# An attention and expert kernel: the second part of its queries, keys and values from a transposed input, and its products of weights and values in twelve sets

## What is computed

```
n = layernorm(x)
q, k, v = Wq n, Wk n, Wv n                    # 16 heads of 16
p = softmax(causal(q k^T / 4))                # per batch and head: 1024 x 1024
x = x + layernorm(Wo (p v))
h = layernorm(x)
w, e = top_2(softmax(h router + bias))
f_e(h) = down_e(act(gate_up_e h + bias_e)) + bias_e
x = x + layernorm(sum over the two experts of w f_e(h))
```

## Time and profile before

| | |
|---|---|
| median of three runs | 1973.35 us |
| profiled execution | 1972.61 us, span 1970.9 us |
| PE busy | 1843.2 us, 94% |
| DVE busy | 1541.8 us, 78% |
| ACT busy | 1310.9 us, 67% |
| POOL busy | 865.1 us, 44% |
| chain that ended last: PE | 84% |

### The profile page before, as it was taken

One profiled execution on the slowest core, in us unless ns is written; L12 is line 12 of the kernel. 1 busy time (PEld: TensorE's weight loads), 2 busy tenths in 40 slices (PEclk: granted clock), 3 DMA queues, 4 the chain that ended last, 5 costly groups with the idle time before them and its releaser, 6 DMA issues.

```text
span 1970.9 us, 75491 instructions
## 1 busy us (share of the span) xinstructions
PE 1843.2 (94%) x26766; PEld 1280.2 (65%) x26767; DVE 1541.8 (78%) x5221; ACT 1310.9 (67%) x3291; POOL 865.1 (44%) x1247
## 2 busy tenths in 40 slices
PE   6899999999999999999999899999999999999980
PEld 3245555555545555455444369999999999999970
DVE  3888888888888888888888658778777777777767
ACT  5177788888888888888787766554445445554437
POOL 4333343445545555555454744544333333333336
PEclk9799999999999999999999999999999999999995
DMA  7744657475655656465557569889899999998848
GB/s 203 219 120 131 196 171 213 150 208 183 184 172 170 189 154 203 137 192 158 167 163 234 169 206 279 240 250 265 252 260 264 257 264 261 264 262 245 239 119 342
DMA packets 255062, 411.72 MB, mean 209 GB/s; under 512 B 34480, under 2 KB 191920, under 8 KB 247600
## 3 DMA queue, kind: packets, MB, share of 16 engines
q1 hardware_dynamic: 217856, 363.46, 57.7%
q0 software_dynamic: 27120, 35.40, 10.2%
q10 hardware_dynamic: 9792, 8.93, 1.5%
HBM read 284.83 MB, written 122.28 MB: 207 GB/s over the span
## 4 chain that ended last, share of the span: by engine, by line
PE 84%; DVE 6%; ACT 4%; issue 3%; DMA 2%; SPq 1%; POOL 0%; DVEq 0%; ACTq 0%; POOLq 0%
PE ps_s L1544 18%; PE ps_s L1375 12%; PE ps_o L1428 12%; PE ps_e L1375 11%; PE ps_w L1375 11%; PE ps_e L1544 6%; PE ps_e L1561 6%; PE ps_o L1561 6%; DVE cmax L792 2%; ACT space L1275 2%; PE ps_e L1554 1%; ACT arena L1167 1%; DVE space L128 1%; PE ps_w L1504 1%; PE ps_w L1441 1%
## 5 line engine op out<-in xcount | busy, mean ns | idle before, releaser
L1167 ACT ACTIVATE arena<-ps_e 128x512 f32<-128x512 f32 (+3 forms) x1536 | 675.5, 498 | 191.8 <-PE ps_e L1375 179.0
L789 DVE CUSTOM_DVE_ANT_0 arena<-ps_s,c 128x384 bf16<-128x384 f32 (+3 forms) x1024 | 461.7, 485 | 117.2 <-PE ps_s L1375 113.5
L1375 PE MATMUL ps_e<-arena 98*32 98x512 bf16 (+3 forms) x6144 | 505.2, 327 | 28.2 <-ACT arena L1167 27.3
L1375 PE MATMUL ps_s<-arena 96*32 96x512 bf16 (+3 forms) x6144 | 509.0, 333 | 10.7 <-DVE rmax L789 3.7
L792 DVE TENSOR_REDUCE cmax<-ps_s 128x1 f32<-128x512 f32 x512 | 322.5, 680 | 28.9 <-PE ps_s L1375 28.1
L1375 PEld LDWEIGHTS ps_s<-arena 96*32 96x32 bf16 x6144 | 177.8, 96 | 211.7 <-DVE rmax L789 80.8
L1428 PE MATMUL ps_o<-arena 128*32 128x512 f32 (+3 forms) x3072 | 296.3, 486 | 6.1 <-ACT ot L1181 3.2
L1375 PEld LDWEIGHTS ps_e<-arena 98*32 98x32 bf16 x6144 | 177.7, 96 | 178.8 <-issue 82.0
L669 POOL DMA_INDIRECT acc<-blank,place_now x135 | 213.3, 1580 | 140.6 <-POOL place_now L662 66.1
L1544 PE MATMUL ps_s<-arena 128*128 128x128 f32 x2192 | 268.5, 276 | 0.8 <-ACT arena L1314 0.7
L1544 PEld LDWEIGHTS ps_s<-arena 128*128 128x128 f32 x2192 | 261.4, 192 | 8.4 <-issue 3.2
(11 more groups left out here) (182 smaller groups left out, 2714.5 us busy)
## 6 DMA issues: line engine op xcount, KB each, us to landing
arena<-in_gate_up SPq DMA_DIRECT2D x91, 1024.0 KB, 6.0
arena<-qk_parts SPq DMA_DIRECT2D x384, 128.0 KB
c_h<-in_gate_up SPq DMA_DIRECT2D x44, 1024.0 KB
qk_parts<-space SPq DMA_DIRECT2D x120, 192.0 KB, 4.4
d_xin<-xs SPq DMA_DIRECT2D x136, 130.5 KB, 3.4
arena<-v_aug SPq DMA_DIRECT2D x32, 512.0 KB, 5.0
o_t<-ot SPq DMA_DIRECT2D x64, 256.0 KB
v_aug<-space SPq DMA_DIRECT2D x28, 512.0 KB, 5.6
```

The source lines that it names most:

```text
L789: dve.tensor_tensor_reduce(summed[:, m % RJ, 0:w], ps_s[:, m % RS, 0:w], after[:, HALF - w:HALF], 1.0, LOWEST, ALU.add, ALU.max, rmax[:, p ...
L1167: act.activation(pw[:, at % RP, begin:end], ps_e[:, n % RE, 0:w], ACT.Exp, scale=SCALE).then_inc(e_done, 1)
L1375: last = pe.matmul(out[at:at + QUAD], lhsT[:, at:at + QUAD], rhs, start=start, stop=stop)
```

## The change

Two things are changed.

**Pairs 6 to 31.** The host also hands over `x` transposed (`x_turned`). ACT no longer normalises `xn`, PE no longer transposes it, and ACT no longer copies it. Instead SP stores `a_rstd` and `a_shift` of the pair (512 numbers) to memory (`norms`, slot 8 of the quad before), loads the transposed rows and then the numbers, broadcast to 128 partitions (both slot 10 of the quad before), and POOL multiplies and adds in place (slot 1). `q_or_k` and its parts start one slot earlier (`Q_AT`). Pairs 0 to 5 are as before.

**Weights times values.** Each chunk is weighed by itself at the end of the slot after its own; chunks 5 to 8 in two halves of 256 columns, one after step 2 and one at the end. ACT copies `ps_o` out one step earlier (`head_out`). Each chunk has its own place in `pw`.

```diff
+    Q_AT = [start if a < FIRST_EVEN else start - 1 for a, start in enumerate(A_AT)]
...
+                for a in due(A_AT, -12, g):
+                    if a >= FIRST_EVEN:
+                        sp.wait_ge(a_shifted, a + 1)
+                        sp.dma_start(norms_v[a], a_norm[:, a % 2].rearrange("p z c -> p (z c)"), allow_slow_non_contiguous=True).then_inc(norms_out, 16)
+                for a in due(A_AT, -10, g):
+                    if a >= FIRST_EVEN:
+                        u = a % 2
+                        sp.wait_ge(a_v, a - 1)
+                        sp.wait_ge(a_xt, a)
+                        sp.dma_start(xn_t[:, u], turned_v[a]).then_inc(turned_in, 16)
+                        sp.wait_ge(norms_out, (a - FIRST_EVEN) * 16 + 16)
+                        if a == FIRST_EVEN:
+                            sp.wait_ge(a_tps, FIRST_EVEN)
+                        sp.dma_start(norm_rows, norms[a:a + 1].broadcast_to([P, 2, WIDE])).then_inc(turned_in, 16)
...
-                for u, (at, done_by, n) in enumerate(((BEGIN - 2, a_p3, 2 * EARLY + 2), (BEGIN + 6, a_p3, 2 * EARLY + 4), (BEGIN + 9, a_p3, 2 * EARLY + 4))):
+                for u, (at, done_by, n) in enumerate(((BEGIN - 2, a_p3, 2 * EARLY + 2), (BEGIN + 6, a_p3, 2 * EARLY + 4), (BEGIN + 9, a_xt, FIRST_EVEN + 1))):
...
+                for a in due(A_AT, -7, g):
+                    if a >= FIRST_EVEN:
+                        u, mine = a % 2, xn_t[:, a % 2]
+                        pool.wait_ge(turned_in, (a - FIRST_EVEN) * 32 + 32)
+                        pool.tensor_tensor(mine, mine, norm_rows[:, 0:1].broadcast_to([P, KT, WIDE]), ALU.mult).then_inc(a_scaled, 1)
+                        pool.wait_ge(a_scaled, a - FIRST_EVEN + 1)
+                        pool.tensor_tensor(mine, mine, norm_rows[:, 1:2].broadcast_to([P, KT, WIDE]), ALU.add).then_inc(a_xt, 1)
...
-                        for a in due(A_AT, 0, g):
+                        for a in due(A_AT[0:FIRST_EVEN], 0, g):
                             act.wait_ge(a_tps, a + 1)
...
-                        for a in pairs_due(-2, -10, g):
+                        for a in due(A_AT[0:FIRST_EVEN], -2, g):
                             u = a % 2
                             act.wait_ge(a_shifted, a + 1)
...
-                        for a in due(A_AT, 2, g):
+                        for a in due(Q_AT, 2, g):
                             first_part(a, 0)
...
+                at, begin, end = q0 % HALF, w * part // parts, w * (part + 1) // parts
                 for s in range(4):
-                    last = pe.matmul(ps_o[s * QUAD:(s + 1) * QUAD, at:at + w], vs[:, u, j, s], pw[:, (entry_of(g) * 4 + s) % RP, begin:end],
+                    last = pe.matmul(ps_o[s * QUAD:(s + 1) * QUAD, at + begin:at + end], vs[:, u, j, s], pw[:, (g * 4 + s) % RP, begin:end],
                                      start=(j == 0), stop=(c + 1 in (FIRST, NE)))
...
+            def apart_of(g):
+
+                return 2 if g % NE not in (0, FIRST) and EXPC[g % NE][2] == HALF else 1
...
                     if s == 2:
-                        for a in due(A_AT, 3, g):
+                        for a in due(Q_AT, 3, g):
                             q_or_k(a, 1, (0,))
+                        if 0 < g <= NE * QUADS and apart_of(g - 1) == 2:
+                            weigh(g - 1, 0, 2)
...
-                for chunks in TOGETHER:
-                    if 0 < g <= NE * QUADS and (g - 1) % NE == chunks[-1]:
-                        for c in chunks:
-                            last = weigh((g - 1) // NE * NE + c)
-                        last.then_inc(pv_done, 1)
+                if 0 < g <= NE * QUADS:
+                    weigh(g - 1, apart_of(g - 1) - 1, apart_of(g - 1))
```

More of the change, by code:

```diff
@@ L153, in combine_stage, with attention_layer @@
     return on_sync, on_gpsimd, on_scalar, on_vector
-def attention_layer(nc, x, wq_t, wk_t, wv_t, wo_t, router_t, router_bias, qk_parts, v_aug, o_t, rden, x1, xs, acc, consts, ident_b, after,
+def attention_layer(nc, x, x_turned, wq_t, wk_t, wv_t, wo_t, router_t, router_bias, qk_parts, v_aug, o_t, rden, norms, x1, xs, acc, consts, ident_b, after,
                     constants_in, kept, expert_weights, w_dn_in, biases_in, gate_up, arena, x1_all, x1_in, load_x1, out):
@@ L170, in attention_layer @@
     RS, RE, RP, RJ = 3, 3, 16, 4
[L171 to L176, removed]
     LOWEST = -3.0e38
@@ L214, in attention_layer @@
     Q_STORES = 4
[L216 to L231, removed]
     const32, const16, c32, c16, consts_in = constants_in
@@ L379, in attention_layer @@
         scattered = [sem(f"scattered{u}") for u in range(2)]
-        base_set, sel_set, zero_at_ready, zeros_out, chain, tables = (sem("g_" + n) for n in ("base_set", "sel_set", "zero_at", "zeros", "chain", "tables"))
+        base_set, zero_at_ready, zeros_out, chain, tables = (sem("g_" + n) for n in ("base_set", "zero_at", "zeros", "chain", "tables"))
         x_in = [sem(f"d_x_in{s}") for s in range(RX)]
@@ L393, in attention_layer @@
         x_v = x.rearrange("b (j c p) d -> (b j) p c d", c=2, p=P)
+        turned_v = x_turned.rearrange("(k p) (a t) -> a p k t", p=P, t=WIDE)
+        norms_v = norms.rearrange("a z (c p) -> a p (z c)", p=P)
         x1_v = x1.rearrange("(n c p) d -> n p c d", c=2, p=P)
@@ L733, in _ @@
                     pool.tensor_tensor(x1_sb[:, u], y[:, u], cx[:, u], ALU.add).then_inc(c_x1, 1)
[L734 removed]
+                for a in due(Q_AT, 6, g):
                     third(a, 1)
[L736 removed]
+                for a in due(Q_AT, 3, g):
                     third(a, 0)
@@ L770, in _ @@
             for sel in sels.values():
-                dve.memset(sel[:], 0.0).then_inc(sel_set, 1)
+                dve.memset(sel[:], 0.0).then_inc(base_set, 1)
             for e in range(E):
@@ L1091, in _ @@
                             place(n, 0)
-                        for a in due(A_AT, 2, g):
+                        for a in due(Q_AT, 2, g):
                             remainder(a, 0)
-                        for a in due(A_AT, 4, g):
+                        for a in due(Q_AT, 4, g):
                             remainder(a, 1)
@@ L1162, in exponential @@
                 n = g * 4 + s
-                at, (begin, end) = entry_of(g) * 4 + s, columns_of(g)
-                if s == 0 and begin == 0 and entry_of(g) >= RP // 4:
-                    act.wait_ge(pv_done, sets_to(entry_of(g) - RP // 4))
+                if s == 0 and g >= RP // 4:
+                    act.wait_ge(pv_done, g - RP // 4 + 1)
                 act.wait_ge(e_scores, n + 1)
-                act.activation(pw[:, at % RP, begin:end], ps_e[:, n % RE, 0:w], ACT.Exp, scale=SCALE).then_inc(e_done, 1)
+                act.activation(pw[:, n % RP, 0:w], ps_e[:, n % RE, 0:w], ACT.Exp, scale=SCALE).then_inc(e_done, 1)
             def high(n):
@@ L1176, in head_out @@
             def head_out(quad, k):
-                act.wait_ge(pv_done, quad * NG + (FIRST_SETS if k == 0 else NG))
+                act.wait_ge(pv_done, quad * NE + (FIRST if k == 0 else NE))
                 if quad >= 1:
@@ L1410, in exp_scores, with weigh @@
                            start=True, stop=True).then_inc(e_scores, 1)
-            def weigh(g):
+            def weigh(g, part, parts):
                 quad, c = divmod(g, NE)
@@ L1662, in ffn_attention_kernel @@
     o_t = scratch("o_t", [B * H // 4, P, S])
+    norms = scratch("norms", [T // 256, 2, 256])
     rden = scratch("rden", [T // 256, H, 256])
```

65 lines of the change are left out of this document (33 added, 32 removed).

## The result

The changed kernel takes 2143.14 us (median of four runs, 2139.56 to 2151.00); the kernel before takes 1973.19 us beside it. The ratio is 1.0859, 95% interval 1.0840 to 1.0879: 170 us more, where 6 were forecast. The profiled execution of the changed kernel has a span of 2143.4 us.

A forecast was written before the change was run, and what follows sets the result against it. PE was taken to set the pace, with DVE and ACT nearly full. Terms -3.5 -1.5 -3.5 +14.8 = +6.3 us on 1972.61 gave 1978.9, 1979.6 beside the runs; the forecast's own range 1971 to 1989, overall 1954 to 1998.

The forecast's parts named there:

- the store of `norms`: Before slot 0: the store between the loads moves their landing from 89.8 to 90.3 us, bounds 87.6 and 94.
- Before slot 0: POOL's product, sum and memset for pair 6 stand ahead of `mpart`, PE waits: +14.8 us, bounds 12 and 19.
- Slot 10: PE waits 1.06 us for ACT's fourth exponential behind `first_part` and two `c_y`, in the 22 pairs from quad 4 on.
- Slots 0 and 1: Less cover, and `remainder` ahead of the 384-wide maxima: PE stalls 0.58 and 0.20, with 0.18 for ACT, together 0.96 us.
- Smaller terms: Weighing chunk 1 earlier and halves in slots 6 to 9 win 0.4 us per quad from quad 4 on, between 0 and 0.8.
- The steady sum: Terms in the quads: -3.5 us in quads 4 to 25, -1.5 in quads 0 to 3, -3.5 in quads 26 to 31.
- Rival 1: The new waits of slot 10 and slots 0 and 1 don't come: one covered 1955 us, both 1932; chance 18%.
- rival 2: Before slot 0 the loads land before POOL is needed, so no hold-up: 1965 us; chance 9%.
- Rival 3: POOL becomes the bound, product and sum delaying the cut of chunk 2: 2000 us at one further us; chance 13%.
- Rival 4: Weight loads don't hide, eight more for each of 128 wide chunks: 112 us slower, 2091 us; chance 1%.
- The direction: Whole kernel: slower 51%, faster 29%, same 20%; slower meant above 1977.3 us.

The follow-up runs named there:

- e1: Changed kernel with the same numbers stored in another order, as 128 pieces of 16 bytes for each pair and not 512 of 4: 1992.4 us, ratio 1.0091.
- e8: e6 plus, behind each store of `norms`, a second store nobody reads, 512 pieces of 4 bytes 512 bytes apart: 1952.8 us.
- e9: e6 plus, behind each store of `norms`, a second store nobody reads, 512 pieces of 4 bytes beside each other in 2 KB: 2121.4 us.
- e5: e1 with pair 6 normalised by ACT and turned by PE as in the kernel before: 1980.3 us, ratio 1.0020.
- e4: Changed kernel without the turned input: only the new weights times values sets, no `norms`, `Q_AT` as before: 1973.5 us, ratio 0.9998.
- e7: e6 with the eight weights times values sets of the kernel before put back: 1955.8 us, ratio 0.9894.
- e6: e5 with q and k of every turned pair one slot later, where the kernel before had them: 1955.1 us, ratio 0.9887.

## Why the prediction was wrong, point by point

**The step that failed: the store of `norms`.** In "Before slot 0" I gave it half a microsecond (90.3 for 89.8), bounded what hangs on it by the 2.3 us of a 16 KB transfer, and wrote that the rule on strided stores would put the load "later in the bounds, not outside". In the quads I did not cost it at all. It measured 14.15 us in the chain, and the numbers landed at 98.55, outside my bound of 94. Its hold makes nearly all of the loss: changed kernel less e1, 140.5 us in quads 0 to 30 (1167.7 - 1027.2) and 12.1 before slot 0 (125.5 - 113.4), 152.6 together (two stores before slot 0, one in each of quads 0 to 23, 5.9 us each). Two errors are in it. An operation without a row was bounded by a transfer of more bytes, though it differs in the one respect that counts, 512 pieces of 4 bytes side by side. And the bound was for the store's own landing, as if nothing else would feel it: before slot 0 the packets behind it took 0.48 us on average, for 0.035 in the kernel before, and in each quad PE stopped. By which way the hold reaches PE stays open.

A part of those 14.15 us is not the pieces: in e1, with 16-byte pieces, the same place in the chain still takes 7.96, behind the loads and stores that SP had issued. There most of it hides: SP is busy with other issues until 85.4, and the row load goes out at 86.7.

```profile
78.75 7.96 DMA norms<-a_norm
```

**The rule I cited, and the one I passed over.** The Trainium skill, "DMA: Bandwidth & Descriptors", Rules for kernel authors, was right that a strided last dimension becomes one descriptor per element: the trace has 528 packets for the 512 numbers. Its section Specifications says that below 512 B a transfer does a read-modify-write. The runs narrow that: 512 such writes 512 bytes apart cost nothing to be seen (e8), and 512 in one stretch of 2 KB cost 166 us over 25 stores (e9), 6.6 us each. No run shows a read-modify-write itself.

**Before slot 0, right.** Without the hold (e1) `mpart` ends at 99.0 and slot 0 starts 15.9 us later than before, where 14.8 were forecast; e5 takes 15.6 back. `mpart` itself is 2.3 later than forecast: the numbers land at 91.9 and not 90.3, and product and sum take 1.5 each with their step of 16 bytes. The two issues of SP that were put at about 0.6 us each, below both neighbours named for them (0.77 and 5.22/4), took 0.76 and 0.34. The mechanism stands, and its size within the 3 us by which that start differs between runs.

**Slot 10, right.** Forecast 1.06 us. The timeline of PE in quad 24 of the changed kernel: the set for the maxima starts at 1108.64 and takes 0.06, the next starts at 1109.76, a stall of 1.06.

```profile
1108.64 0.27 PE L1377 MATMUL ps_s<-arena 96*32 96x128 bf16 x4
1109.76 0.24 PE L1377 MATMUL ps_e<-arena 98*32 98x128 bf16 x4 [0.85 <-ACT arena L1171]
```

ACT shows the order that was forecast, `first_part` and two `c_y` ahead of the fourth exponential of 256 columns:

```profile
1107.87 0.59 ACT L1195 ACTIVATE space<-ps_w 128x512 bf16<-128x512 f32 x1
1108.34 1.09 ACT L1289 ACTIVATE c_y<-c_y,c_shift,c_rstd 128x256 f32<-128x256 f32 x2
1109.33 1.00 ACT L1171 ACTIVATE arena<-ps_e 128x256 f32<-128x256 f32 x4
```

**Slots 0 and 1, right.** Forecast 0.96. In slot 0 of quad 24:

```profile
1081.39 0.34 PE L1377 MATMUL ps_s<-arena 96*32 96x384 bf16 x4
1081.71 0.35 PE L1377 MATMUL ps_e<-arena 98*32 98x384 bf16 x4
1082.42 0.35 PE L1377 MATMUL ps_s<-arena 96*32 96x384 bf16 x4 [0.36 <-DVE rmax L794]
```

1.03 us for two sets of 0.17: 0.69 (forecast 0.18 of ACT and 0.58 of DVE), and 0.24 by the same count in slot 1.

**Smaller terms, half wrong.** The 0.40 us a quad from spreading was 0.15 (slots 3 to 8 lose 1.08 us before and 0.93 in e5). In quads 9, 13, 17 and 21, in which the routing of a batch is worked out as well, slot 2 waits over a microsecond for DVE: 37.0 us where they took 35.4, 6.3 us in all that I had not looked for. Quads 1 to 3 (31.5 for 31.9) and 26 and 27 (28.7 for 29.4) came as forecast; quad 0 of e5 is 1.1 longer. The steady sum was -8.5 us; e5 against before gives +4.3 in quads 0 to 30. So without the hold too (e1, 1992.4) the time would have been above my own range of 1971 to 1989, by these terms.

**The rivals.** Rival 1 (no new stalls) and rival 2 (no hold-up) fall. Rival 3 was slower through POOL: product and sum took 1.27 and 1.26 us, as the earlier trace rows had it, and in quad 24 PE does not wait for a cut. Rival 4 falls: a half takes 0.43 us, the forecast's figure (e4). None named an effect of one transfer on all the others. The direction would have held without it (e1 is 0.9% slower, most of it by the start); of the size nine tenths come from what no rival had.

## What to carry to other kernels

An operation that no row shows is not bounded by a row that only has its bytes: ask in what it differs, and leave the far end open until one run has shown it. Where all engines stop at once and the profile names no releaser, look at what the DMA engines were given just before, and make a run that differs in that alone. Test a suspected way from cause to effect in the same trace: instruction loads looked like the link here, and one quad without any was enough to speak against it. Before a small strided store is taken into a loop, lay its destination out so that each partition writes one piece; in these runs pieces that begin 16 bytes apart were nearly free, and 4 bytes apart dear.

## What the runs showed of the hardware that was not expected

- 512 pieces of 4 bytes into 2 KB of memory slow the packets behind them, and PE, DVE and ACT stop for up to 7 us (8 in e9); the same pieces 16 bytes apart cost some 0.2 to 0.3 us a store ((1959.6 - 1955.1) / 25, or 0.0034 of 1973 by the ratios / 25), 512 bytes apart nothing to be told from noise. Writes that queue up at one small block of memory would look like this; no run shows the memory itself.
- In these stops PE's sets are done by its timeline, but their semaphores rise 1.6 to 7.1 us later (60 waits of the changed kernel).
- A lump of weights times values moves a wait and does not remove it: with it in slot 0, slot 11 waits (e7, 32.8 us a quad), without it slot 1 does (e6, 32.6).
- POOL's product and sum, which read their row of numbers with a step of 16 bytes and a shape of one more dimension, are a quarter to a third slower: 1593 and 1662 ns (e1) for 1278 and 1275.
